# Row-by-row gathers on SyncE and ScalarE: one tile of 48 each instead of one of 64

## The reference, cut to what matters

```python
h = relu(layernorm(x)); x = x + (1 + eps) * h + segment_sum(h[src] * edge_weight[:, None], dst)   # L0
h = relu(relu(layernorm(x)) @ W_node + b_node)                                                    # L1
for i in range(3):
    h = gru(segment_sum(ew[:, None] * (h @ conv[i])[src], dst), h)       # ew = sum(z * edge_attr)
x = x + h
h = relu(layernorm(x)); x = x + relu(segment_sum(alpha[rel] * (h @ w_rel[rel])[src], dst) + ...)  # L2
h = relu(layernorm(x)); x = x + (h + segment_sum(h[dst], src) / deg) @ W.T + b                    # L3
```

## Time and profile before

| what | value |
|---|---|
| median of 3 runs | 6412.83 us (6412.31 to 6414.54) |
| profiled execution, its own time | 6415.0 us |
| its span, first to last instruction | 6413.2 us |
| POOL busy | 4678.5 us (73%) |
| DVE busy | 3857.3 us (60%) |
| PE busy | 3385.5 us (53%) |
| ACT busy | 685.4 us (11%) |

### The profile page before, as it was taken

How to read it: one execution, slowest core, us unless ns; L and a number is a source line. 1 busy time by engine, 2 the same in 40 slices (tenths; PEclk the granted TensorE clock), 3 DMA queues, 4 the chain that set the end, 5 groups by cost and what they waited for, 6 DMA issues and landing times.

```text
span 6413.2 us, 126206 instructions
## 1 busy us (share of the span) xinstructions
PE 3385.5 (53%) x13756; PEld 2711.3 (42%) x13756; DVE 3857.3 (60%) x13960; ACT 685.4 (11%) x1522; POOL 4678.5 (73%) x4958
## 2 busy tenths in 40 slices
PE   3444445555557565555656554695454444444444
PEld 2333334444444454445445553443343333333334
DVE  6767666666666666767677774454464445444445
ACT  1000002000002000000200000143333333000000
POOL 6777776777774677777777777676777776777775
PEclk6555556666667766766866765696555555555556
DMA  5443342222222222222222222263222222222222
GB/s 140 111 111 109 108 112 78 59 61 60 60 59 66 59 59 59 61 59 56 68 60 59 59 61 59 86 233 116 54 54 54 54 54 56 56 55 56 56 56 60
DMA packets 284171, 472.88 MB, mean 74 GB/s; under 512 B 104795, under 2 KB 181466, under 8 KB 277067
## 3 DMA queue, kind: packets, MB, share of 16 engines
q0 software_dynamic: 154640, 302.91, 18.6%
q1 hardware_dynamic: 89755, 94.70, 4.5%
q10 hardware_dynamic: 38944, 67.15, 3.0%
HBM read 379.46 MB, written 86.91 MB: 73 GB/s over the span
## 4 chain that ended last, share of the span: by engine, by line
POOL 39%; issue 22%; SPq 15%; DMA 12%; PE 7%; DVE 3%; ACT 1%; ACTq 1%; DVEq 0%; POOLq 0%
POOL G L744 36%; SPq L605 12%; DMA G<-h_rows,ix_src 9%; PE ps L848 7%; SPq L597 3%; POOL by_src L769 3%; DMA G<-h_rows 1%; DMA G<-t_rows,pos 1%; ACTq L1926 1%; DVE HNA L1322 0%; POOL rstd L760 0%; SPq L618 0%; DVEq L1311 0%; ACT gate L1982 0%; DVE M L1302 0%
## 5 line engine op out<-in xcount | busy, mean ns | idle before, releaser
L744 POOL DMA_INDIRECT G<-h_rows,ix_src x3812 | 3618.2, 949 | 1270.0 <-issue 1022.9
L848 PE MATMUL ps<-G,M 128*128 x10000 | 2507.5, 414 | 2860.1 <-SPq L618 1957.5
L848 PEld LDWEIGHTS ps<-G,M 128*128 128x128 f32 x10000 | 2129.0, 304 | 3296.3 <-issue 3290.4
L1322 DVE TENSOR_TENSOR HNA<-HNA,ps 128x128 f32 (+1 forms) x3328 | 957.7, 288 | 1244.5 <-PE ps L848 1212.8
L1302 DVE TENSOR_SCALAR M<-irow,rel,w_l 128x128 f32<-128x128 f32 x3328 | 1201.8, 364 | 177.1 <-issue 170.5
L744 POOL DMA_INDIRECT G<-t_rows,pos x770 | 735.9, 956 | 253.2 <-issue 226.5
L1322 DVE TENSOR_TENSOR HTA<-HTA,ps 128x129 f32 x840 | 243.5, 290 | 502.0 <-PE ps L848 493.2
L848 PE MATMUL ps<-sorting 128*128 128x128 f32 x1568 | 428.2, 369 | 0.0
L2021 ACT ACTIVATE G<-G,pk 128x128 f32<-128x128 f32 x782 | 312.1, 402 | 671.3 <-DMA G<-t_rows,pos 668.8
L1322 DVE TENSOR_TENSOR X<-X,ps 128x128 f32 x832 | 239.1, 287 | 234.2 <-PE ps L848 231.4
L848 PEld LDWEIGHTS ps<-sorting 128*128 128x128 f32 x1568 | 361.1, 283 | 0.0
(11 more groups left out here) (277 smaller groups left out, 2163.4 us busy)
## 6 DMA issues: line engine op xcount, KB each, us to landing
G<-h_rows SPq DMA_DIRECT2D x7680, 0.5 KB
G<-h_rows ACTq DMA_DIRECT2D x6144, 0.5 KB
G<-h_rows,ix_src POOLq DMA_INDIRECT x3812
t_rows<-G SPq DMA_DIRECT2D x33, 1024.0 KB, 4.4
HTA<-in_edge_attr_n ACTq DMA_DIRECT2D x50, 500.0 KB
HTA<-in_edge_attr ACTq DMA_DIRECT2D x50, 500.0 KB
G<-t_rows SPq DMA_DIRECT2D x1536, 0.5 KB
t_rows<-sorting SPq DMA_DIRECT2D x16, 1024.0 KB, 4.6
```

The source lines that it names most:

```text
L744: return nc.gpsimd.indirect_dma_start(to, None, table, bass.IndirectOffsetOnAxis(ap=ix, axis=0))
L848: return nc.tensor.matmul(dst, lhsT, rhs, start=start, stop=stop, skip_group_check=True)
L1322: V.tensor_tensor(to, to, ps[:, u % SLOTS, 0:n], ALU.add).then_inc(s_add, 1)
```

## The change

One tile of 48 is fetched row by row in place of one of 64 (`PER = 48`): 16 tiles a pass by SP, and in the same four passes 16 by ACT. The row lists hold byte offsets: DVE shifts them left by 9, and the DMA's source is the table seen as one line of bytes. SP's tiles get four slots of their own behind the 64 of the ring and ACT's two (`G` grows from 66 to 70 slots). SP spreads a tile's 128 rows over 11 of the 12 groups of four tiles, not over all. The slot list takes longer arithmetic and moves out of `steps_of` into `slots_of`; at the start of the kernel that stands behind `signal(s_ix)`. SP's first wait is for DVE's shift (`s_off`). Some small tensors are laid over others (`aw1`, `cnt`, `ew_r`) to make room, two loads of `aw1` move from ACT to SP, and ACT's `attend` loop covers 192 tiles instead of 128.

```diff
-BY_ROW = RING - 1
-BY_ACT = RING - 2
-ROW_SETS, ROW_PARTS = 3, 4
-ROW_SET = ROW_PARTS * RING
-ROWS_A_QUAD = P * QUAD // RING
+PER = 48
+BY_ROW = PER - 1
+BY_ACT = PER - 2
+ROW = 4 * D
+ROW_BITS = 9
+ROW_SETS, ROW_PARTS = 4, 4
+ROW_SET = ROW_PARTS * PER
...
-            return t % RING == BY_ROW or (t % RING == BY_ACT and k in ACT_PASSES)
+            return t % PER == BY_ROW or (t % PER == BY_ACT and k in ACT_PASSES)
...
+        def by_bytes(table):
+
+            return table.bitcast(U8).rearrange("n c -> (n c)").rearrange("(o c) -> o c", o=1)
 
         def slot_of(t):
 
-            return t % RING + (2 * (t // RING % 2) if t % RING >= BY_ACT else 0)
+            n = t // PER + 1
+            return {BY_ACT: RING + n % 2, BY_ROW: RING + 2 + n % 4}.get(t % PER, t % RING)
...
-            def row_slot_free(k, c, j):
-
-                done = k * S + (j - 2) * RING + BY_ROW + BLK
+            def row_slot_free(k, c, j, slots=4):
+
+                done = k * S + (j - slots) * PER + BY_ROW + BLK
                 sp.wait_ge(s_mm, max(done, 1) + c * ROW_SET)
...
-            def fetch(k, j, q, table, row):
-                for e in range(q * ROWS_A_QUAD, (q + 1) * ROWS_A_QUAD):
-                    sp.dma_start(G[e:e + 1, BY_ROW + 2 * (j % 2), 0:D], table[bass.ds(row[e % RD], 1), :]) \
-                        .then_inc(s_row[k // 2][j % 2], 16)
+            def fetch(k, c, j, e0, e1, table, listed, row):
+                for e in range(e0, e1):
+                    if e % RD == 0:
+                        row = row_numbers(listed, c, j, e, table.shape[0])
+                    sp.dma_start(G[e:e + 1, slot_of(j * PER + BY_ROW), 0:D].bitcast(U8),
+                                 by_bytes(table)[:, bass.ds(row[e % RD], ROW)]).then_inc(s_row[k][j % 2], 16)
+                return row
...
-                            fetch(k, j, q, table, row)
-                        one(c, j * RING + BY_ROW)
+                            row = fetch(k, c, j, P * min(q, quads - 1) // (quads - 1), P * min(q + 1, quads - 1) // (quads - 1),
+                                        table, listed, row)
+                        one(c, j * PER + BY_ROW)
...
-            sp.wait_ge(s_ones, 16 * 2 * ROW_PARTS)
+            sp.wait_ge(s_off, 1)
             sp.wait_ge(s_hst, 16 * stores(N0))
             arrivals(PASS_L0, ET, EF, h_rows, one_by_one)
...
-                    row_slot_free(PASS_L2, c, j)
...
+                    row_slot_free(PASS_L2, c, j, 2)
+                    fetch(PASS_L2, c, j, 0, P, t_rows, one_by_one, None)
...
+            def slots_of(steps, to_b, to_bb, tau, t1, t2):
                 at = slice(ROW_SLOT, ROW_SLOT + 32)
...
+                link(V.scalar_tensor_tensor(own, to_bb[at, 0:steps], -1.0, srow[at, 0:steps], ALU.mult, ALU.add))
+                V.tensor_copy(to, own)
+                link(V.tensor_scalar(n, own, 2.0, 683.0, ALU.add, ALU.mult))
+                link(V.tensor_single_scalar(n, n, 15, ALU.logical_shift_right))
+                link(V.scalar_tensor_tensor(behind, n, -float(PER), own, ALU.mult, ALU.add))
+                link(V.tensor_scalar(own.bitcast(I32), behind, 2.0, 5.0, ALU.mult, ALU.add))
+                link(V.tensor_tensor(n, n, own.bitcast(I32), ALU.bitwise_and))
+                V.tensor_single_scalar(to, to, RING - 1, ALU.bitwise_and)
+                link(V.scalar_tensor_tensor(own, behind, 2.0, n, ALU.mult, ALU.add))
+                link(V.scalar_tensor_tensor(own, own, RING + 4.0, to, ALU.add, ALU.subtract))
+                link(V.scalar_tensor_tensor(own, behind, 0.0, own, ALU.is_lt, ALU.mult))
+                link(V.tensor_tensor(to, to, own, ALU.add))
                 at = slice(ROW_TILE, ROW_TILE + 32)
...
             signal(s_ix)
+            slots_of(S, b_i, bb, tau, tau1, tau2)
...
+            dve.wait_ge(s_ones, 16 * 2 * ROW_PARTS)
+            V.tensor_single_scalar(one_by_one[:], one_by_one[:], ROW_BITS, ALU.logical_shift_left)
+            V.tensor_single_scalar(act_by_one[:], act_by_one[:], ROW_BITS, ALU.logical_shift_left).then_inc(s_off, 1)
             lead_in(PASS_L0, rel, w_l)
...
-            steps_of(key3, T3_TB, T3_NB, S3, 2, 6, b3_i, bb3, tau3)
+            steps_of(key3, T3_TB, T3_NB, S3, 2, 6, b3_i, bb3)
+            slots_of(S3, b3_i, bb3, tau3, gate[:, S3:2 * S3], gate[:, 2 * S3:3 * S3])
...
-                    act.dma_start(G[q * RD + e:q * RD + e + 1, BY_ACT + 2 * (j % 2), 0:D], h_rows[bass.ds(row[e], 1), :]) \
-                        .then_inc(s_rowa[k // 2][j % 2], 16)
+                    act.dma_start(G[q * RD + e:q * RD + e + 1, slot_of(j * PER + BY_ACT), 0:D].bitcast(U8),
+                                  by_bytes(h_rows)[:, bass.ds(row[e], ROW)]) \
+                        .then_inc(s_rowa[k][j % 2], 16)
 
             def slot_free(k, j):
 
-                act.wait_ge(s_mm, k * S + (j - 2) * RING + BY_ACT + BLK)
+                act.wait_ge(s_mm, k * S + (j - 2) * PER + BY_ACT + BLK)
```

More of the change, by code:

```diff
@@ L12 @@
 U32 = mybir.dt.uint32
+U8 = mybir.dt.uint8
 P = 128
@@ L621, in arrivals @@
                     for j in range(ROW_PARTS):
[L622 to L623 removed]
+                        row, quads = None, PER // QUAD
+                        for q in range(quads):
+                            t = j * PER + q * QUAD
                             for u in range(QUAD):
[L625 removed]
+                                if (t + u) % PER != BY_ROW:
                                     one(c, t + u)
@@ L853, in one_round @@
                     lists[ROW_SLOT:ROW_SLOT + 1, bass.ds(r * RD, steps)], engines=[mybir.EngineType.PE],
-                    min_val=0, max_val=RING + 1,
-                    skip_runtime_bounds_check_because="a slot is a tile's number modulo RING, or one of the two behind")
+                    min_val=0, max_val=RING + 5,
+                    skip_runtime_bounds_check_because="a slot is a tile's number modulo RING, or one of the six behind")
                 _, upto = nc.values_load_multi_w_load_instructions(
@@ L1208, in _, with steps_of @@
             link(V.memset(note[:], 0.0))
-            def steps_of(key, tb, nb, steps, k0, k1, to_b, to_bb, tau, beside=None):
+            def steps_of(key, tb, nb, steps, k0, k1, to_b, to_bb, beside=None):
                 for t in range(nb):
@@ L1220, in steps_of @@
                 V.tensor_copy(to_b[ROW_B:ROW_B + 32, :], to_bb[ROW_B:ROW_B + 32, :])
+            def slots_of(steps, to_b, to_bb, tau, t1, t2):
                 at = slice(ROW_SLOT, ROW_SLOT + 32)
[L1222 to L1229, removed]
+                n, behind, to = t1[at, 0:steps].bitcast(I32), t2[at, 0:steps], to_b[at, 0:steps]
+                own = tau[at, 0:steps]
+                link(V.scalar_tensor_tensor(own, to_bb[at, 0:steps], -1.0, srow[at, 0:steps], ALU.mult, ALU.add))
[10 more added lines that the diff above has]
+                link(V.tensor_tensor(to, to, own, ALU.add))
                 at = slice(ROW_TILE, ROW_TILE + 32)
@@ L2008, in _, with attend @@
             A.activation(alog[:, 1:2], alog[:, 0:1], ACT.Sigmoid, bias=ab2[:]).then_inc(s_att, 1)
[L2011 to L2012 removed]
+            def attend(i, n, more=0):
                 for u in range(n):
                     if u % QA == 0:
[L2015 to L2021 removed]
+                        act.wait_ge(s_aw, i * (ROW_SET // QA) + u // QA + 1)
+                    if u % PER == BY_ROW:
+                        j = u // PER
+                        act.wait_ge(s_row[PASS_L2][j % 2], 16 * P * (i * (ROW_PARTS // 2) + j // 2 + 1))
+                    else:
+                        v = u % RD
+                        act.wait_ge(s_g[v], 16 * (used(PASS_L2, v) + i * nth_use(PASS_L2, ROW_SET + v) + nth_use(PASS_L2, u) + 1))
+                    A.mul(G[:, slot_of(u), 0:D], G[:, slot_of(u), 0:D], a_l[:, bass.ds(i * ROW_SET + u, 1)]) \
                         .then_inc(s_arr[PASS_L2], 1 if u < n - 1 else 1 + more)
[L2024 to L2027 removed]
+            with act.Fori(0, ROW_SETS) as i:
+                attend(i, ROW_SET)
+            attend(ROW_SETS, EF - ROW_SETS * ROW_SET, ET - EF)
             def n2_out(i):
```

84 lines of the change are left out of this document (35 added, 49 removed).

## The result

The changed kernel takes 6454.1 us, the median of 4 runs (6453.0 to 6460.3). The kernel before took 6412.6 us on the same chip (4 runs, 6409.5 to 6414.5). The ratio is 1.0067 with an interval of 1.0055 to 1.0078: 0.7% slower, where 0.5% faster was forecast. The profiled span is 6452.7 us, 39.5 longer than before.

The account below looks back on a forecast made before the run. POOL's gathers were taken as the bound: -50.2 for gathers, -3.5 at the start, +9.6 in L0, +8.8 in L1a, +4.6 in L2, +0.5 added operations make -30.2; 6412.8 becomes 6383 us, 8 in 10 for 6355 to 6405.

Parts of the forecast that it names:

- What SP must now do: SP per 48 tiles: rows, loads and counts make 55.3 us, under POOL's 57.5 by 2.2, so SP keeps up.
- A pass is as long as its number of gathers: Inside a pass POOL never really waits; 40 gathers fewer at 1.25 us save 50.2 us.
- Rival 2: ACT or SP falls behind in L1b, L1c and L3 as well: 6408 us, from 6397 to 6420; chance 0.12.
- Rival 1: The stalls at the starts of L0 and L1a and in L2 do not come: 6360 us; chance 0.14.
- Rival 3: The register instruction stays or another replaces it, SP becomes the bound at 0.41 us a row: 6950 us; chance 0.09.
- Rival 4: Transfers, not their issue, set the pace, so fewer gathers save no time: 6433 us; chance 0.03.
- The first gather: At the kernel's start, POOL's first gather moves forward by 3.5 us from 54.97, to near 51.5.
- the stall at tile 64: In L0 POOL waits 9.6 us for step 52, which moves by 9.7 us to 141.6.
- The first product: At the start of L0, longer slot arithmetic and list shifts move PE's first product from 63.9 to 70.7.
- the counts of tiles 28 to 31: In L0 SP's rows start late, so these tiles count at about 107, where before they were let through at 94.
- the three stalls: POOL's waits: 9.6 us in L0, 8.8 in L1a with SP's 3 more, 4.6 in L2.
- rival C: From the experiments, not the prediction: landings are slow because more rows are under way, and whoever waits is late; no chance given.

Follow-up runs that it names:

- experiment 7: The kernel before, counting its row tile behind the first 8 rows of the next and SP's loop over the sets written out: 6416.9 us, ratio 1.0004.
- experiment 2: The changed kernel with one row tile of 64 again (`PER = 64`), byte offsets and slot arithmetic kept: 6420.0 us, ratio 1.0004 to the kernel before.
- experiment 3: The changed kernel with offsets in elements instead of bytes, so the register instruction of each row stays: 7041.5 us in one run.
- experiment 5: The changed kernel with SP's loop written out and all 16 row tiles counted after the next tile's first 11 rows: 6394.5 us, ratio 0.9967.
- experiment 10: The edits of experiment 8 and experiment 9 together: 6375.3 us, ratio 0.9937 to the kernel before.
- experiment 6: As experiment 5, but SP's first rows in L0 don't wait for PE's first step: 6395.2 us, ratio 0.9969 to the kernel before.
- experiment 8: As experiment 6, with DVE's two shifts of the row lists ahead of its slot arithmetic: 6386.9 us, ratio 0.9959 to the kernel before.
- experiment 9: As experiment 5, but in L1a ACT issues 64 rows of its first tile before waiting for the sorting's list: 6383.7 us, ratio 0.9952.
- experiment 4: The changed kernel with SP's loop over the four sets of tiles written out as straight code: 6419.7 us, ratio 1.0003 to the kernel before.

## Why the prediction was wrong

**The step that failed** is the sum in "What SP must now do": 128 x 0.336 + 8.8 + 3.5 = 55.3. Its three terms were right within 0.5 us: over 15 cycles of L1b the rows took 42.5 us a cycle, the loads 8.7 with the register work ahead of them, and the counts 3.7 with theirs. But the sum holds only what SP issues, and not what it waits for. SP counts its own row tile right behind its last row, so once in each cycle it stands for that row's landing, 3.1 us on the mean. The prediction gave ACT's rows in L1a "about 2 us to land" and put SP's at nothing. And the loop's end, 2.65 once in four cycles, was not in it either. 55.3 + 3.1 + 0.7 = 59.1; from the first load of L1b's first row tile at 2140.80 to that of the sixteenth at 3025.82 it is 885.0 / 15 = 59.0. The margin was 2.2 and the missed terms 3.8.

The kernel before waited for such landings too, 114 us in all, but by the prediction's own count (66 of 77.5) it had 11 us to spare for them in each cycle, and experiment 7 shows that they cost nothing there. At its price of 1.75 us the sum would still have come to only 55.3 + 1.75 + 0.7 = 57.75, hardly over 57.5. What made SP clearly the bound is that the landing also grew, to 3.1, and that no row of before shows. Closer rows alone don't do it: in experiment 2 they follow one another as closely, and the wait is 1.4.

**A second error hid the first.** "A pass is as long as its number of gathers" is true of POOL, and I looked for SP's lag as a wait of POOL in mid-pass. There is hardly one (the longest is 1.3 us, at tile 80 of L1a): POOL may be 28 tiles ahead of SP's counts, and in a pass SP falls back by 15 x 1.5 = 22 us, some 18 tiles. The lag comes out behind the last gather, where PE still has to step through what SP counts late. In L1b SP's last count comes at 3082.0, 5.3 us behind POOL's end; for the other 13.4 us of the tail PE and DVE step through the tiles that were let through last. L2 is the test within the run: there ACT counts, and the tail is 5.1 us as before.

**Rival 2** named the mechanism, with a chance of 0.12, but its price was capped at the 10 us a pass that POOL saves, and it left out L0 and L1a. A lag isn't capped by what another engine saves: in L1b SP's costs 13.8 us, where POOL saved 10.2. **Rival 1** (no stalls) falls with the stalls below. **Rival 3** would have been 6950 by its price of 0.41; experiment 3 measured 7041.5, with gathers' stretches near the 1054 reckoned, and the tails on top. **Rival 4** falls by the gathers' stretches, shorter by 10 us in each of L1b, L1c and L3: the transfers don't set the pace.

**What was right**, with rows of after. POOL's first gathers and the one at tile 64 of L0:

```profile
52.60 1.04 POOL L751 DMA_INDIRECT G<-h_rows,ix_src  x1 [7.88 <-DMA h_rows<-HNA]
...
144.66 0.94 POOL L751 DMA_INDIRECT G<-h_rows,ix_src  x1 [12.38 <-PE ps L855]
```

The first gather came at 52.6 (forecast 51.5) and the stall at tile 64 is 12.1 (9.6). Its chain held too. PE at the start of L0, beside the earlier trace rows:

```profile
70.50 2.07 PE L855 MATMUL ps<-G,M 128*128 x8 [12.35 <-DVE M L1318]
...
107.13 2.07 PE L855 MATMUL ps<-G,M 128*128 x8 [2.04 <-SPq L625]
```

The first product was forecast for 70.7, the counts of tiles 28 to 31 for about 107. In L1a ACT and POOL, beside the earlier trace rows:

```profile
1114.65 49.97 ACTq L1949 DMA_DIRECT2D G<-h_rows  x128
...
1168.71 0.94 POOL L751 DMA_INDIRECT G<-h_rows,ix_src  x1 [6.27 <-PE ps L855]
```

ACT's first tile took 52.2 us with the first load's 2.2 (forecast 51.7). The pass begins 13.6 us later than before; less that, tile 64 comes at 1155.1, where 1155.2 was forecast, and the stalls there sum to 8.8, as forecast. In L2, beside the earlier trace rows:

```profile
4762.13 0.95 POOL L751 DMA_INDIRECT G<-t_rows,pos  x1 [2.91 <-PE ps L855]
```

The stalls there are 3.2 us at tiles 272 and 276 (forecast 4.6), and L2 gained nothing. The gathers' stretches and the start together came to -27.4, where the forecast had -30.7 for them. So nearly the whole miss is the tails. With SP's two missed costs taken away and the stalls left in, experiment 5 gains 20 of the forecast 30 us. The 6375 of experiment 10 needs two of the three stalls cut as well, which the forecast had kept.

**What stays open.** Why the landings grow. In experiments 5, 6, 8, 9 and 10 L1c's tails are 9.2, 6.7, 7.9, 5.4 and 8.7, and SP's waits there for its own rows 25.9, 17.8, 23.0, 15.0 and 22.7 us: the long tail goes with late landings. In the trace of experiment 5 the DMA packets of SP's rows begin 1.0 us behind their instructions in the first eighth of L1c and 6.8 in the seventh; in the kernel before it is 0.9 to 1.0 all through L1c. So rows pile up behind their issue, as rival C has it, in that pass at least; what holds them back, no run shows. Nor does one show what sets the remaining stall in L0.

## What to carry to other kernels

When an engine is to keep up with another by a few per cent, sum its cycle from one start to the next in the trace, not from the instructions that it issues: waits that it already has, harmless as long as it is ahead, belong in the sum once its slack is gone, and they can grow with the change, as the landing did from 1.75 to 3.1 us. Where a queue lets one engine run ahead of another, a lag shows first at the end of the stage and not as a wait in its midst, so follow the stage to the last instruction of the last engine. A wait for one's own transfer goes behind the next piece of issuing; that one edit turned 0.7% slower into 0.2% faster.

## What the runs showed of the hardware

**The landing of one row.** For the last of 128 rows of 512 bytes, each a DMA of its own, SP stood 3.1 us on the mean, and 1.75 in the kernel before. From the start of the row's instruction to its landing it was 4.85 and 3.22 in the rows above. The DMA engines were busy for 0.24 of L1b. The Trainium skill ("DMA: Bandwidth & Descriptors", section "Anatomy of one DMA — SWDGE (gpsimd) path") gives a DMA of GpSimd about 2.0 us of fixed time, most of it the wait until the target memory confirms the write. These rows are issued by SP and not by GpSimd, and the changed kernel's trace shows more: the measured 3.1 us decides.

**The end of a loop.** In SP's loop the branch at line 627 took 0.05 us, and 2.65 us followed in which SP waited for nothing that the profile shows. With the loop written out, which spares register work too, the tails became 36 us shorter (experiment 4). The Trainium skill ("Advanced Engine Details and Errata", section "Control Flow Timing") has about 108 ns for a compare-and-branch. The trace doesn't agree for the stretch behind this one. At each of the 15 ends of a turn in the changed kernel that go back to the loop's start, 2.4 to 2.7 us follow the branch, once 5.0. In each of these stretches a packet of 8192 bytes starts on a DMA queue that the profile calls "instruction", 0.9 to 1.1 us behind the branch, and 3.3 behind it in the one of 5.0. So SP seems to stand for its instructions; no run tests it.

**A register instruction a row.** With offsets in elements a row carries an instruction of 33 ns more; the 225 ns of the DMA and the 29 of the move stayed, and rows start 0.39 us apart instead of 0.32 (medians of L1b). The kernel took 7041.5 us with it and 6454.1 without, and POOL then waited 487 us for SP.
